# A graph network on one core: 183 scatters of edge counts moved behind the last merge, landed by eights, with block-by-block waits in layer 2

## The reference, cut to what matters

```python
x = _layernorm(x + _L0(x, edge_index, edge_attr_16, ...))
x = _layernorm(x + _L1(x, edge_index, ...))       # four attention passes a, b, c, d
x = _layernorm(x + _L2(x, W, b, w_ih, w_hh, ..., src, dst, edge_type_4))
x = _layernorm(x + _L3(x, weight, edge_weight1, src, dst, edge_type_16))

def _L1(...):   # _gat: softmax of the edges of each node, weighted sum of h[src]
    h = relu(_bn(_gat(x, src, dst, We1, ...)))        # a, 8 heads x 16
    enc = _gat(h, src, dst, We2, ...)                 # b, 8 heads x 32
    h2 = relu(_bn(_gat(enc, src, dst, Wd1, ...)))     # c, 8 heads x 16
    return _gat(h2, src, dst, Wd2, ...)               # d, 8 heads x 64

def _L2(feat, ...):
    h = feat
    for _ in range(5):
        h_all = einsum('nd,ted->nte', h, W) + b
        m = h_all[src, etypes]
        a = segment_sum(m, dst, num_segments=n_nodes)
        h = _gru_cell(a, h, w_ih, w_hh, b_ih, b_hh)
    return h
```

## Time and profile before

| | us |
|---|---|
| median of 3 runs (8886.32 to 8889.57) | 8888.87 |
| the profiled execution, its own time | 8891.25 |
| its span | 8890.0 |
| pass d, first to last gather | 4783.3 to 6250.6 |
| end of the merge of pass d | 6436 |
| first counts of layer 2 on TensorE | 6500.66 |
| last counts of step 0 | 6754.8 |

### The profile page before, as it was taken

How to read it: one execution, slowest core, us unless ns; L and a number is a source line. 1 busy time by engine, 2 the same in 40 slices (tenths; PEclk the granted TensorE clock), 3 DMA queues, 4 the chain that set the end, 5 groups by cost and what they waited for, 6 DMA issues and landing times. The chain is left out here.

```text
span 8890.0 us, 111137 instructions
## 1 busy us (share of the span) xinstructions
PE 5328.1 (60%) x39647; PEld 4855.0 (55%) x39647; DVE 4045.6 (46%) x8424; ACT 2223.2 (25%) x5853; POOL 5594.2 (63%) x5805
## 2 busy tenths in 40 slices
PE   4545624545466667344455677676889999933323
PEld 3333424445366666344444666676679999923323
DVE  7666524443444444566664445454422222233333
ACT  0000013333133332233322444444111111021221
POOL 7777677777777777777777777777510000057776
PEclk8777667777588886677776888888689999966665
DMA  7665252222244441343333555555178888821111
GB/s 240 207 198 180 47 54 62 63 62 57 53 115 116 114 116 41 108 120 113 116 80 105 151 152 152 151 152 151 24 292 325 329 329 326 331 77 27 27 27 27
DMA packets 440766, 1203.87 MB, mean 135 GB/s; under 512 B 161729, under 2 KB 235330, under 8 KB 399570
## 3 DMA queue, kind: packets, MB, share of 16 engines
q1 hardware_dynamic: 203188, 707.03, 22.8%
q0 software_dynamic: 237024, 489.72, 22.5%
HBM read 1072.84 MB, written 120.95 MB: 134 GB/s over the span
## 5 line engine op out<-in xcount | busy, mean ns | idle before, releaser
L1264 PE MATMUL ps<-pool 128*106 128x128 f32 (+2 forms) x19344 | 2571.4, 301 | 5.3 <-DVE pool L1164 5.3
L1264 PEld LDWEIGHTS ps<-pool 128*106 128x106 f32 (+2 forms) x19344 | 2547.9, 185 | 8.4 <-DVE pool L1164 5.6
L1222 ACT ACTIVATE ACC<-ps 72x256 f32 (+1 forms) x2418 | 1010.4, 418 | 1990.4 <-PE ps L1264 1745.9
L482 POOL DMA_INDIRECT ACC<-t,ACC x416 | 392.5, 944 | 1490.2 <-DVE ps L1793 1363.7
L1243 PE MATMUL ps<-ident,pool 128*128 128x128 f32 (+1 forms) x204 | 90.7, 445 | 1882.3 <-DVE pool L1122 1882.3
L1243 PEld LDWEIGHTS ps<-ident,pool 128*128 128x128 f32 (+1 forms) x204 | 36.9, 181 | 1921.1 <-issue 1921.1
L764 POOL DMA_INDIRECT cnt_d<-pool x806 | 833.3, 1034 | 320.7 <-issue 234.3
L1122 DVE COPY pool<-pool 128x128 f32<-128x128 f32 (+1 forms) x204 | 46.8, 229 | 1967.7 <-DMA pool<-d_h,srcT_s 663.1
L1291 POOL DMA_INDIRECT pool<-a_h,srcT_s x806 | 776.1, 963 | 245.5 <-issue 244.9
L1164 DVE TENSOR_TENSOR pool<-pool,ps 128x1024 f32<-128x1024 f32 (+1 forms) x807 | 928.3, 1213 | 0.0
L1291 POOL DMA_INDIRECT pool<-d_h,srcT_s x806 | 772.2, 958 | 245.6 <-issue 198.0
(11 more groups left out here) (300 smaller groups left out, 6601.2 us busy)
## 6 DMA issues: line engine op xcount, KB each, us to landing
ACC<-cnt_d SPq DMA_DIRECT2D x172, 1600.0 KB, 8.7
pool<-cnt_d SPq DMA_DIRECT2D x88, 1600.0 KB, 8.7
cnt_d<-pool SPq DMA_DIRECT2D x26, 3200.0 KB
ACC<-key_d SPq DMA_DIRECT2D x31, 1792.0 KB
ACC<-key_d SPq DMA_DIRECT2D x25, 2048.0 KB, 8.1
pool<-seg_d SPq DMA_DIRECT2D x100, 129.0 KB
cnt_d<-pool POOLq DMA_INDIRECT x806
pool<-a_h,srcT_s POOLq DMA_INDIRECT x806
```

The lines of the kernel that those rows point to most:

```text
L482: g.indirect_dma_start(out=gb[b][:, k, :], out_offset=None, in_=table, in_offset=bass.IndirectOffsetOnAxis(ap=idx[:, c:c + 1], axis=0)).th ...
L1222: a.activation(win[:, 0:NPL, bass.ds(reg, 128)], pl[0].rearrange("p (i c) -> p i c", c=128), ACT.Copy).then_inc(*(tile_out if last else A) ...
L1264: mm = t.matmul(o, gbr[:, tile % RT, M * i:M * i + M], oh, start=True, stop=True)
```

## The change

The scatters of pass d are spread in another way: 163 between the gathers where there were 345, 16 and 48 behind them as before, then two for each merged block (62) where there was one, and then 183 where there were 32. The last 183 cover odd tiles from tile 441 on, so the counts of the first blocks are complete without them. They run in 23 chunks of eight (the last has seven) on two semaphores in turn. After chunk k is issued, GpSimd waits for chunk k - 1 to land and then counts up `late_done` by a small memset. Before the first chunk it waits for all earlier scatters. VectorE works out in pass a, from the slot numbers, how many ticks each block needs (`need`), and in step 0 SyncE loads that number into a register ahead of the first half of each block and waits for it. The last block waits for all.

The weights of layer 2 and layer 3 are loaded by SyncE behind the shares of pass d's merge. VectorE clears `wnn` ahead of `vector_wholes` and adds the biases in the merge, and the row of ones in `xT` is written by GpSimd. The second barrier stays, with next to nothing between it and the first, and the index list for layer 3 is worked out behind the first eight table rows.

```diff
-        EARLY, TAIL_, BESIDE, MERGED, AFTER, LATE = 25, 16, 48, NS, 8, 24
+        EARLY, TAIL_, BESIDE, MERGED, AFTER = 25, 16, 48, NS, 8
         GAP = TAIL_ + BESIDE + MERGED + AFTER
+        BESIDE_D, MERGED_D, LATE_D, CHUNK = 48, 2 * NS, 183, 8
+        GAP_D = TAIL_ + BESIDE_D + MERGED_D + LATE_D
+        LATE_0, CHUNKS_D = NT // 2 - LATE_D, LATE_D // CHUNK + 1
...
-                    in_=cval[:, c:c + 1], in_offset=None).then_inc(*counted.one())
+                    in_=cval[:, c:c + 1], in_offset=None).then_inc(*(done or counted).one())
+
+        def gpsimd_late_counts(s0):
+            g.wait_ge(*counted.now())
+            g.memset(tick[:, 0:1], 0.0).then_inc(*late_done.one())
+            for k in range(CHUNKS_D):
+                scatter_counts(s0 + CHUNK * k, min(s0 + CHUNK * (k + 1), NT), late[k % 2])
+                if k:
+                    g.wait_ge(*late[(k - 1) % 2].now())
+                    g.memset(tick[:, k:k + 1], 0.0).then_inc(*late_done.one())
+            g.wait_ge(*late[(CHUNKS_D - 1) % 2].now())
+            g.memset(tick[:, CHUNKS_D:CHUNKS_D + 1], 0.0).then_inc(*late_done.one())
...
+                v.tensor_scalar(passed[0:1, 0:NS2], upto0[0:1, :], 2.0, float(1 + CHUNK - LATE_0), ALU.mult, ALU.add).then_inc(*V.one())
...
+                v.tensor_scalar(need, passed[0:1, 0:NS2], 0.0, float(CHUNK), ALU.max, ALU.add).then_inc(*V.one())
+                v.wait_ge(*V.now())
+                v.tensor_scalar(need, need, 3, None, ALU.logical_shift_right).then_inc(*V.one())
+                mark["need"] = V.now()
...
-            p0, p1 = EARLY + GAP * layer, NT - GAP - LATE
+            p0, p1 = EARLY + GAP * layer, NT - GAP_D
...
             def gpsimd_merge():
-                s0 = (p0 if layer < 3 else p1) + TAIL_ + BESIDE
+                s0, each = (p0 + TAIL_ + BESIDE, 1) if layer < 3 else (p1 + TAIL_ + BESIDE_D, 2)
+                if layer == 3:
+                    g.wait_ge(share_out.sem, sh0 + 48)
+                    g.memset(xT[D:D + 1, :], 1.0).then_inc(*const.one())
                 for b in range(NS):
                     g.wait_ge(slot_mm.sem, smm0 + b + 1)
-                    scatter_counts(s0 + b, s0 + b + 1)
-                scatter_counts(s0 + NS, s0 + NS + AFTER if layer < 3 else NT)
+                    scatter_counts(s0 + each * b, s0 + each * (b + 1))
+                s0 += each * NS
+                if layer < 3:
+                    scatter_counts(s0, s0 + AFTER)
+                else:
+                    gpsimd_late_counts(s0)
...
                 if following is not None:
                     sync_weights(*following)
+                else:
+                    sync_l2_weights()
...
+                if layer == 3:
+                    vector_l2_zeros()
                 vector_wholes()
...
+                    if layer == 3 and j == 4:
+                        vector_l2_biases()
...
         def sync_counts(stp):
             if stp == 0:
                 s.wait_ge(*counted.now())
+                s.wait_ge(*mark["need"])
             for b, h in ORDER:
                 u = half_of(stp, b, h)
+                if stp == 0 and h == 0:
+                    if b < NS2 - 1:
+                        s.wait_ge(late_done.sem, s.value_load(need[0:1, b + 1:b + 2], min_val=1, max_val=CHUNKS_D + 1))
+                    else:
+                        s.wait_ge(*late_done.now())
                 if u >= NR:
                     s.wait_ge(half_mm.sem, u - NR + 1)
...
             if stp == 0:
                 v.memset(acc[0:D, :], 0.0).then_inc(*V.one())
                 vector_rows(0, 0, AHEAD)
+                vector_l3_lists()
```

More of the change, by code:

```diff
@@ L121, in build @@
         rel2, pidx, win2 = pool[:, 21830:21830 + NS2], pool[:, 21860:21861], pool[0:1, 21870:21870 + NS2].bitcast(I32)
+        need, tick = pool[0:1, 21900:21900 + NS2].bitcast(I32), pool[0:1, 21930:21990]
         first2, low = aux[:, 0:NB].bitcast(I32), aux[:, NB:2 * NB].bitcast(I32)
@@ L154, in build @@
         filled, flag0, flagged, counted = dsig("cnt_filled"), dsig("flag_zeroed"), dsig("flagged"), dsig("counted")
+        late = [dsig("late_counts0"), dsig("late_counts1")]
+        late_done = sig("late_chunks_done")
         counted_ready, odd_ready = sig("counts_ready"), sig("odd_counts_ready")
@@ L751, in tensor_l0_end, with scatter_counts @@
                 mm.then_inc(*t2v.one())
-        EARLY, TAIL_, BESIDE, MERGED, AFTER, LATE = 25, 16, 48, NS, 8, 24
+        EARLY, TAIL_, BESIDE, MERGED, AFTER = 25, 16, 48, NS, 8
         GAP = TAIL_ + BESIDE + MERGED + AFTER
-        def scatter_counts(c0, c1):
+        BESIDE_D, MERGED_D, LATE_D, CHUNK = 48, 2 * NS, 183, 8
+        GAP_D = TAIL_ + BESIDE_D + MERGED_D + LATE_D
+        LATE_0, CHUNKS_D = NT // 2 - LATE_D, LATE_D // CHUNK + 1
+        assert LATE_D % CHUNK == CHUNK - 1
+        def scatter_counts(c0, c1, done=None):
             for i in range(c0, c1):
@@ L1600, in batchnorm, with vector_l2_zeros, vector_l2_biases, sync_l2_weights @@
             barrier()
+        w2, w3_in = dsig("w2_in"), dsig("w3_in")
+        wc, wzr, wnn = wl[0:D + 1, 0:256], wl[:, 256:384], wl[:, 384:512]
+        bih, bhh, brz = wl[:, 512:515], wl[:, 515:518], wl[:, 518:520]
+        w3 = wl[:, 520:1544]
+        def vector_l2_zeros():
+            v.memset(wnn, 0.0).then_inc(*V.one())
+            mark["wnn"] = V.now()
+        def vector_l2_biases():
+            v.wait_ge(*w2.now())
+            v.tensor_tensor(out=brz, in0=bih[:, 0:2], in1=bhh[:, 0:2], op=ALU.add).then_inc(*V.one())
+        def sync_l2_weights():
+            s.wait_ge(*mark["wnn"])
+            s.dma_start(wc[0:D, :], I["L2_W"][:, :]).then_inc(*w2.one())
+            s.dma_start(wc[D:D + 1, :], I["L2_gnn_b"].rearrange("t e -> (t e)").unsqueeze(0)).then_inc(*w2.one())
+            for p0, x in ((0, "L2_wih"), (D, "L2_whh")):
+                s.dma_start(wzr[p0:p0 + D, 0:D], I[x][:, D:2 * D]).then_inc(*w2.one())
+                s.dma_start(wzr[p0:p0 + D, D:2 * D], I[x][:, 0:D]).then_inc(*w2.one())
+                s.dma_start(wnn[p0:p0 + D, p0:p0 + D], I[x][:, 2 * D:3 * D]).then_inc(*w2.one())
+                s.dma_start(bih[p0:p0 + D, :], I["L2_bih"][:, :]).then_inc(*w2.one())
+                s.dma_start(bhh[p0:p0 + D, :], I["L2_bhh"][:, :]).then_inc(*w2.one())
+            for p0 in (0, D):
+                s.dma_start(w3[p0:p0 + D, :], I["L3_W"][:, :]).then_inc(*w3_in.one())
         gat("a", 64, 16, None, (128, 32, I[L + "We2"], I[L + "as_e2"], I[L + "ad_e2"]),
@@ L1613, in build @@
         barrier()
-        idx_in, w2 = dsig("idx_in"), dsig("w2_in")
+        t.wait_ge(*const.now())
+        t.wait_ge(*w2.now())
+        idx_in = dsig("idx_in")
         for dst_, src_ in ((ew, "ewT"), (idx16, "et16T")):
             s.dma_start(dst_, I[src_][:, :]).then_inc(*idx_in.one())
[L1619 to L1624, removed]
+        both = acc4[:, 0, :]
         r_, z_, n_ = (gates[:, 512 * j:512 * (j + 1)] for j in range(3))
@@ L1642, in build, with vector_l3_lists @@
         half_mm, y_sum, merge_mm, win_add = sig("half_mm"), sig("slot_sum"), sig("merge_mm"), sig("window_add")
[L1644 to L1652, removed]
-                s.dma_start(bhh[p0:p0 + D, :], I["L2_bhh"][:, :]).then_inc(*w2.one())
-        def vector_l2_zeros():
-            v.memset(wnn, 0.0).then_inc(*V.one())
-            mark["wnn"] = V.now()
-        def vector_l2_prep():
+        def vector_l3_lists():
             v.wait_ge(*idx_in.now())
@@ L1662, in vector_l2_prep @@
                                    op1=ALU.add).then_inc(*V.one())
-            v.wait_ge(*w2.now())
-            v.memset(xT[D:D + 1, :], 1.0).then_inc(*V.one())
-            v.tensor_tensor(out=brz, in0=bih[:, 0:2], in1=bhh[:, 0:2], op=ALU.add).then_inc(*V.one())
-            mark["w2"] = V.now()
-        vector_l2_zeros()
-        sync_l2_prep()
-        for p0 in (0, D):
-            s.dma_start(w3[p0:p0 + D, :], I["L3_W"][:, :]).then_inc(*w3_in.one())
-        vector_l2_prep()
         barrier()
```

2 lines of the change are left out of this document (1 added, 1 removed).

## The result

| | before | after |
|---|---|---|
| median, us | 8887.6 (8885.14 to 8889.57, 4 runs) | 8616.27 (8610.88 to 8622.59, 4 runs) |
| the profiled execution, own time / span | 8891.25 / 8890.0 | 8614.48 / 8613.1 |

The changed kernel takes 0.9696 of the time before, with a 95% interval of 0.9685 to 0.9708: 271 us less. The forecast was 8621 us.

The account below looks back on a forecast made before the run. Pass d was taken to run at GpSimd's issue pace, with TensorE the bound in step 0. Span: 8890.0 - 242 - 28 + 1 - 2 + 3 = 8622; forecast median 8621 us, own range 8606 to 8636, 8-in-10 range to 8670.

Parts of the forecast that it names:

- Pass d: Pass d: 182 scatters fewer between the gathers, 1.33 us each, save 242 us; the pass takes 1225 us.
- The room of the ring: Pass d: the ring of 32 tiles still leaves gathers 7 us of room at the faster pace.
- Rival 3: Pass d: ring or TensorE keeps groups at 27 us or more, gain only 106 us, kernel 8757; chance 5%.
- Start of step 0: From merge to first counts: early weights and no wait for the last 32 scatters start counting 27.9 us earlier.
- Small terms: Start of step 0: index list between table rows costs +1 us; TensorE's clock rising sooner gives -2 us.
- The late scatters: Behind the merge, beside step 0: 183 scatters, memsets and delays last 245 us, last issue at 6692.
- The room was put at 9 us: End of step 0: block 24's load lands 9 us before TensorE needs it.
- The 3 us of waiting in the sum: Step 0: 3 us allowed for TensorE possibly waiting on late scatters.
- Rival 1: Step 0: VectorE or loads slow late scatters, TensorE overtakes them; 8633 to 8670 us, chance 18% for 8636 to 8680.
- Rival 2: Step 0: chunks land slowly under loads, 15 us each, 91 us lost, kernel 8712; chance 4%.
- Rival 4: Step 0: late scatters beside loads cost 3.0 instead of 1.27 us each, kernel 8889 or more; chance 2%.
- The signs: Trace marks: pass d's last gather at 6008, first counts 36 us behind merge's last scatter, no `cnt_d` waits in blocks 14-25.

Follow-up runs that it names:

- e8: Changed kernel with the 163 scatters left inside pass d omitted, so their edges are missing from the counts: 8393.73 us in one run.
- e2: Changed kernel with the loads of layer 2's weights and their setup put back between the two barriers, all scatters staying late: 8628.52 us.
- e4: Changed kernel with 32 more scatters behind the last merge (215 instead of 183), 131 left in pass d: 8604.42 us.
- e3: Changed kernel with SyncE waiting for all 183 late scatters before the first load of counts, instead of block by block: 8836.91 us.
- e7: Changed kernel with the late scatters in chunks of four instead of eight: 8617.07 us.
- e9: Kernel e5 with eight more late scatters (199 instead of 191), 139 left in pass d: 8597.15 us.
- e5: Changed kernel with eight more scatters ahead of the wait for the last tiles and eight more behind the merge (191 late): 8594.24 us.

## Why the prediction was right

- *Pass d* (242 us, pass at 1225). Measured 242.9 and 1224.4. The price of 1.33 us a scatter, taken from the difference between a pass with scatters and one without, holds down to zero: e8 has 217 us less in the pass for 163 scatters, 1.33 again. The room of the ring, worked out as 7 us at the new pace, was enough: no gather waited.
- *Rival 3* (ring or TensorE holds the pass) falls by e8. The estimate with TensorE's 20.2 us a group was even too careful, since those 20.2 us were taken at the lower clock.
- *Start of step 0* (27.9 us). Measured 27.6 us. It was put together from 13.8 us for the weights and the rest for the scatters; e2 gives 13.6 for the weights by its timeline and 12.3 by the median. The unknown price of a register load is small. One lies ahead of the first load of counts, the second between the first load and the next, and the first lies, with two DMA issues of 0.34 and 0.42 us, in the 1.9 us between 6215.05 and 6216.94. The answer on its line:

```profile
L1924 SPq TENSOR_LOAD <-pool x25: 262/273/472, 6216.1 to 6429.8; - x25
```

  So the 2 us that I took for two of them and two DMAs were about 1 us short, and the load was still in time.
- *Small terms.* The index list cost nothing visible, since it ran on VectorE at 6227.95, behind the start of the counts. Step 0, from its first counts to its last, was 1.5 us shorter, for which -2 had been taken, and the reason was the one given: the clock stood at 0.50 for 9 us of counting instead of 12.
- *The late scatters.* The stretch was put at 245 us and took 241.0. Its parts were less exact: the ticks were priced at 9 us and cost under 1, because a memset of 0.09 us fits into the gap of 0.3 us that follows a scatter anyway; against that one gap of 5.6 us stands in the middle, which had no price. The last chunk landed 9.3 us behind the issue of its last scatter (6439.93 to 6449.21), where about 7 had been taken. The room was put at 9 us and is 9.5, by the 8.0 us of e4: that these errors nearly cancel is luck. The 3 us of waiting in the sum were not needed.
- *The difference that is left.* The profiled span is 8613.1 us and the forecast's was 8622, 8.9 us more. Of these, 3.7 us lie ahead of pass d, where nothing was changed, and so say nothing on the change; 3 and 1 us are the waiting and the index list; the pass gained 0.9 us more than forecast, the stretch from its last gather to the barrier cost 1.1, and 2.2 us lie behind step 0. The two terms of step 0 came out 0.4 and 0.5 us smaller than forecast. The measured gain between the medians is 271 us, the forecast's 268.
- *Rival 1* (scatters slowed by VectorE or by loads). Slower scatters are there: ten of the 183 took more than 1.02 us. Each of them starts inside a VectorE instruction with both inputs in SBUF and ends 0.83 to 0.85 us behind the end of that instruction. The timelines of GpSimd and of VectorE in the changed kernel show a long delay, none, and a short delay:

```profile
6200.20 1.83 POOL L771 DMA_INDIRECT cnt_d<-pool  x1 [0.30 <-issue]
...
6204.19 0.97 POOL L771 DMA_INDIRECT cnt_d<-pool  x1 [0.30 <-issue]
...
6220.28 1.10 POOL L771 DMA_INDIRECT cnt_d<-pool  x1 [0.30 <-issue]
```

```profile
6199.36 1.82 DVE L534 TENSOR_TENSOR xn<-xn,small 128x1600 f32<-128x1600 f32 x1
...
6203.08 1.82 DVE L538 TENSOR_REDUCE small<-pool 128x25 f32<-128x1600 f32 x1
...
6220.12 0.41 DVE L1903 TENSOR_TENSOR pool<-pool 128x256 bf16<-128x256 f32 x1
```

  The scatters of 6200.20 and 6220.28 start inside such an instruction; the one of 6204.19 starts inside a reduction with one input and takes its usual 0.97. So for GpSimd the Trainium skill's rule (SBUF — State Buffer, "two separate sides") and these rows agree. For VectorE they do not: L534 starts at 6199.36, while a scatter runs from 6198.93 to 6199.90, and takes the 1.82 us that L531 took in the earlier trace rows. The price that I worked out by the rule does not hold either: four scatters, beside L534, L536 (1.55 us), L545 (1.80) and the index list (L1705, 1.73), cost 3.0 us together, and six beside the short instructions of step 0 cost 0.8 us together, where 21 us had been the worst case. (That list had even left out L1868 of the kernel before, L1903 now, with another 11 us.) A scatter is held up only by what is left of the instruction when it starts, and most start at another time. The median step between scatters is 1.274 us.
- *Rival 2* (slow landing). Landing does get slower under the loads: 2.1 us without (e3), enough for ticks to wait behind 6.07 us with them (e7). It stays below the 11.2 us that eight scatters cover, even for the last chunk with its 9.3. The Trainium skill's rule on transfers below 512 bytes (DMA: Bandwidth & Descriptors, Specifications) may stand behind that slowing; no run separates it from plain queueing behind the loads, and its price here was nothing.
- *Rival 4* (slower) would have needed 3.0 us a scatter; it is 1.27.
- *The signs.* The last gather of the pass is at 6004.0 (6008 forecast), the last late scatter 39 us ahead of the end of step 0 (35), and no wait of TensorE on `cnt_d` stands in step 0. The first counts are 31 us behind the merge's last scatter, at 6196.48, where 36 had been forecast: with two a block the scatters end behind the merge's matmuls.

## What to carry to other kernels

An engine that only issues one DMA after another is a budget: price a piece by the difference between two stretches with and without it, and move it to where that engine has nothing to do. The DMA engines need not be idle there: the late scatters ran beside loads at a DMA share of 0.92 to 0.94. Work moved behind a consumer's start is free only as far as the consumer asks for it piece by piece (e3: 221 us), and only until the last piece is late (e4, e9); compare the two end times, here tick plus 8.0 us of load against TensorE's arrival, before moving more. A gap of one fixed small length that the profile puts down to another engine is no wait: read the longest column.

## What the hardware showed that I had not expected

- TensorE's granted clock in pass d went from 0.84 to 0.90 and then 0.98 (e8) as the same work came closer together, and its busy time from 997 to 971 and 895 us. Nothing was gained by it, since GpSimd was the bound. The reverse in step 0 of e4 and e9: after waits of 3.5 to 11 us the matmuls ran at half the clock for a while, so such a wait cost 2 to 3 us beyond its own length. Behind the 1.2 us wait of e9 the 52 matmuls took their usual 4.45 us.
- In each kernel with late scatters of this size, the gap ahead of one late scatter is long: 5.63 us in the changed kernel, 5.45 in e5, 6.70 in e7, 1.70 in e3 where no load ran. The profile calls it "issue".

```profile
6351.89 0.97 POOL L771 DMA_INDIRECT cnt_d<-pool  x1 [5.63 <-issue]
```

It is ahead of the 114th late scatter each time, whether 591 scatters (e4) or 623 stand before the late ones, and whether 13 ticks lie among the first 113 late ones or 27 (e7). It gets longer beside the loads. What GpSimd does there was not settled.
- A 1 x 1 memset on GpSimd between two indirect DMAs takes 0.09 us and is swallowed by the gap of 0.30 us between them.
